# Attention kernel on one core: the value products in two column halves, one ahead of score 1 and one ahead of score 3

## What is computed

```python
q, k, v = jnp.split(qkv, 3, axis=2)
att = jnp.einsum('bhqd,bhkd->bhqk', q, k) / np.sqrt(HEAD_DIM).astype(np.float32)
causal = jnp.tril(jnp.ones((T, T), dtype=bool))
att = jnp.where(causal, att, 0.0)
att = jax.nn.softmax(att, axis=-1)
out = jnp.einsum('bhqk,bhkd->bhqd', att, v)
```

## Time and profile before

| | |
|---|---|
| median of 3 runs | 1096.74 us (1095.18 to 1096.81) |
| the profiled execution's own time | 1100.31 us |
| its span, first to last instruction | 1098.1 us |
| mean granted clock of PE | 0.993 |
| PE busy in the span | 1056.5 us (96%) |
| DVE busy | 843.4 us (77%) |
| ACT busy | 698.0 us (64%) |
| POOL busy | 386.7 us (35%) |

### The profile page before, as it was taken

One profiled execution on the slowest core, in us unless ns is written; L12 is line 12 of the kernel. 1 busy time (PEld: TensorE's weight loads), 2 busy tenths in 40 slices (PEclk: granted clock), 3 DMA queues, 4 the chain that ended last, 5 costly groups with the idle time before them and its releaser, 6 DMA issues.

```text
span 1098.1 us, 21867 instructions
## 1 busy us (share of the span) xinstructions
PE 1056.5 (96%) x8064; PEld 531.2 (48%) x8064; DVE 843.4 (77%) x1185; ACT 698.0 (64%) x1487; POOL 386.7 (35%) x945
## 2 busy tenths in 40 slices
PE   5989999999999999999999999999999999999998
PEld 3655555554544454444444444444454445443445
DVE  5667787679779887988898889879987997798023
ACT  2433333267777777777777777777777777777572
POOL 3211211355414451444253335324531553153301
PEclk9999999999999999999999999999999999999799
DMA  3586664455004600540163036104600460011123
GB/s 126 168 255 184 196 216 151 140 86 95 7 8 64 107 2 14 107 61 7 28 104 44 7 45 108 22 7 60 104 12 8 62 105 7 8 56 37 34 90 120
DMA packets 62030, 84.13 MB, mean 77 GB/s; under 512 B 12260, under 2 KB 42212, under 8 KB 60900
## 3 DMA queue, kind: packets, MB, share of 16 engines
q1 hardware_dynamic: 60772, 78.55, 33.0%
q0 software_dynamic: 1152, 4.19, 1.3%
HBM read 44.30 MB, written 34.08 MB: 71 GB/s over the span
## 4 chain that ended last, share of the span: by engine, by line
PE 76%; DVE 16%; issue 3%; ACT 3%; DMA 1%; POOL 0%; SPq 0%; ACTq 0%; DVEq 0%; POOLq 0%
PE ps_o L1156 21%; PE ps_s L1142 21%; DVE part_max L354 11%; PE ps_m L337 8%; PE ps_vr L736 5%; PE ps_qk L727 4%; PE ps_m L1187 3%; ACT probs L1020 3%; PE ps_o L1167 2%; PE ps_m L344 2%; PE ps_xt L770 2%; PE ps_qk L736 2%; PE ps_s L1131 2%; PE ps_pieces L337 1%; PE ps_s L1132 1%
## 5 line engine op out<-in xcount | busy, mean ns | idle before, releaser
L1020 ACT ACTIVATE probs<-ps_s 128x512 f32<-128x512 f32 (+3 forms) x1280 | 599.4, 538 | 233.4 <-PE ps_s L1142 226.7
L354 DVE TENSOR_REDUCE part_max<-ps_m 128x2 f32<-128x1024 f32 (+2 forms) x594 | 614.4, 1058 | 115.3 <-PE ps_m L337 83.2
L1142 PE MATMUL ps_s<-q_op,k_op 50*128 50x512 f32 (+3 forms) x1280 | 436.2, 424 | 7.1 <-ACT probs L1020 3.0
L337 PE MATMUL ps_m<-k_op,q_op 48*128 48x512 f32 (+3 forms) x1188 | 342.7, 413 | 12.5 <-DVE part_max L354 11.1
L1142 PEld LDWEIGHTS ps_s<-q_op,k_op 50*128 50x128 f32 x1280 | 207.1, 186 | 304.0 <-ACT probs L1020 236.1
L972 POOL TENSOR_SCALAR_AFFINE_SELECT probs<-probs 128x128 f32<-128x128 f32 x512 | 145.8, 294 | 453.5 <-ACT probs L1020 444.9
L1156 PE MATMUL ps_o<-probs,v_sb 128*32 128x512 f32 (+3 forms) x2560 | 302.4, 545 | 0.0
L337 PEld LDWEIGHTS ps_m<-k_op,q_op 48*128 48x128 f32 x1188 | 161.5, 185 | 43.9 <-DVE part_max L354 40.2
L938 POOL TENSOR_TENSOR diag_weight<-ident,masked_weight 128x256 f32<-128x256 f32 x256 | 150.4, 624 | 40.6 <-ACT masked_weight L993 40.6
L344 PE MATMUL ps_m<-mask,pick 64*128 64x64 bf16 (+1 forms) x932 | 91.9, 208 | 0.0
L1156 PEld LDWEIGHTS ps_o<-probs,v_sb 128*32 128x32 f32 x2560 | 50.7, 108 | 72.5 <-issue 31.3
(11 more groups left out here) (76 smaller groups left out, 695.7 us busy)
## 6 DMA issues: line engine op xcount, KB each, us to landing
parts_d<-parts SPq DMA_DIRECT2D x32, 512.0 KB, 4.7
q_op<-parts_d SPq DMA_DIRECT2D x84, 128.0 KB, 7.9
k_op<-parts_d SPq DMA_DIRECT2D x84, 128.0 KB, 8.4
vpad_d<-v_pad SPq DMA_DIRECT2D x32, 256.0 KB, 3.5
v_sb<-vpad_d SPq DMA_DIRECT2D x8, 1024.0 KB, 5.8
x_in<-x SPq DMA_DIRECT2D x8, 512.0 KB, 4.9
ffn_d<-ffn SPq DMA_DIRECT2D x8, 512.0 KB, 3.2
attn_t<-normed SPq DMA_DIRECT2D x128, 32.0 KB, 2.0
```

Of the source, the lines that this page charges most:

```text
L337: last = pe.matmul(ps_m[:, f % ring * 2 + e, 0:width], self.q_op[rows, p, j, q0:q0 + P], self.k_op[rows, p, j, pc * CH:pc * CH + width], s ...
L354: dve.tensor_reduce(both, ps_m[:, bank:bank + 2, 0:width], AX_X, ALU.max).then_inc(self.piece_reduced, 1)
L1020: act.activation(probs[:, slot % PRING, 0:width], ps_s[:, bank_of("scores", slot, i * 2 + p), 0:width], ACT.Exp).then_inc(probs_ready, 1)
L1142: pe.matmul(ps_s[:, bank_of("scores", slot, i * 2 + p), 0:CH - q0], k_op[rows, p, h % 2, kt * P:(kt + 1) * P], q_op[rows, p, h % 2, u * CH ...
```

## The change

A step's order is now written as a string: S a score, M a piece, A and B the two halves of W, X as before. The order before was S M S X S M S W. In the new one A handles the query columns 0 to 255 of the unit and B the columns 256 to 511. A tile is not split when it is the first key tile of its unit or when fewer than 257 of its queries are left; then all of it is done at B and nothing at A. At the first three steps of a unit the weighed tile is one of these.

```diff
+ORDER = "SMASXSMBS"
+
+
+def weighed_columns(u, kt, part):
+
+    q0 = first_query(u, kt)
+    if kt == 0 or q0 >= CH // 2:
+        return (q0, CH) if part == 1 else None
+    return (q0, CH // 2) if part == 0 else (CH // 2, CH)
...
-            def weigh_values(p, u, kt, G):
+            def weigh_values(p, u, kt, G, part):
 
                 n = G * NCH + u
+                if weighed_columns(u, kt, part) is None:
+                    return
...
                 q0 = first_query(u, kt)
+                q1, q2 = weighed_columns(u, kt, part)
                 for at, h in enumerate(HEAD_AT):
-                    last = pe.matmul(ps_o[h * HW:(h + 1) * HW, q0:CH], v_sb[:, p, kt, h * HW:(h + 1) * HW],
-                                     probs[:, ((KT0[u] + kt) * GH + at) % PRING, 0:CH - q0],
+                    last = pe.matmul(ps_o[h * HW:(h + 1) * HW, q1:q2], v_sb[:, p, kt, h * HW:(h + 1) * HW],
+                                     probs[:, ((KT0[u] + kt) * GH + at) % PRING, q1 - q0:q2 - q0],
                                      start=(kt == 0), stop=(kt == key_tiles(u) - 1))
-                last.then_inc(probs_used, 1)
+                if part == 1:
+                    last.then_inc(probs_used, 1)
...
-                        for at in range(GH):
-                            score_tile(u, kt, at, i, p, first, last)
...
+                        at = m = 0
+                        for op in ORDER:
+                            if op == "S":
+                                score_tile(u, kt, at, i, p, first, last)
+                                at += 1
...
+                            if op == "X":
                                 between_scores(i, p, u, kt, first, last)
-                            if at == GH - 1:
-
-
+                            if op in "AB":
+                                part = "AB".index(op)
                                 if kt >= LAG:
-                                    weigh_values(p, u, kt - LAG, G)
+                                    weigh_values(p, u, kt - LAG, G, part)
```

More of the change, by code:

```diff
@@ L1170, in masked_keys, with finish_unit @@
                 last.then_inc(masked_done, 1)
-            def finish_unit(p, u, G, step):
-                weigh_values(p, u, key_tiles(u) - LAG + step, G)
+            def finish_unit(p, u, G, step, part):
+                weigh_values(p, u, key_tiles(u) - LAG + step, G, part)
             def output_tile(k):
@@ new lines, in group @@
+                        for op in ORDER:
+                            if op == "S":
+                                score_tile(u, kt, at, i, p, first, last)
+                                at += 1
+                            if op == "M":
+                                some, ahead = pieces_at(u, kt, m)
+                                m += 1
+                                if not (ahead and last):
+                                    for f in some:
+                                        if ahead and f == 0:
+                                            pe.wait_ge(front_loaded[1 - p], ops.loaded(1 - p, i + 1 + p))
+                                        if ahead and f == PIECE0[NCH // 2]:
+                                            pe.wait_ge(back_loaded[1 - p], ops.loaded(1 - p, i + 1 + p))
+                                        ops.score_piece(pe, ps_m, MRING, f, 1 - p if ahead else p, (G + ahead) * PIECES)
+                            if op == "X":
@@ L1228, in group @@
                                 between_scores(i, p, u, kt, first, last)
-                            if at == GH - 1:
+                            if op in "AB":
+                                part = "AB".index(op)
                                 if kt >= LAG:
-                                    weigh_values(p, u, kt - LAG, G)
+                                    weigh_values(p, u, kt - LAG, G, part)
                                 elif u > 0:
-                                    finish_unit(p, u - 1, G, kt)
+                                    finish_unit(p, u - 1, G, kt, part)
@@ L1236, in group @@
                                 elif not first:
-                                    finish_unit(1 - p, NCH - 1, G - 1, kt)
+                                    finish_unit(1 - p, NCH - 1, G - 1, kt, part)
                 if last:
@@ L1240, in group @@
                     for step in range(LAG):
-                        finish_unit(p, NCH - 1, G, step)
+                        for part in range(2):
+                            finish_unit(p, NCH - 1, G, step, part)
                     for k in range(len(OUT_AT), OUTS):
```

## The result

The changed kernel takes 1089.49 us in the median (1088.02 to 1090.59, 4 runs), the kernel before 1096.78 (1095.18 to 1097.92, 4 runs). The ratio is 0.9934 with a 95% interval of 0.9917 to 0.9951: 7.3 us faster. The forecast was 7.3 us slower, and the time lies 0.5 us under the range's lower end.

The account below looks back on a forecast made before the run. The prediction took a loop of PE and ACT waiting for each other as the bound. Seven groups +3.5, first group's extra +0.6 and last group +3.2 gave +7.3 us: 1096.7 to 1104.0 us, range 1090 to 1113.

Parts of the forecast that it names:

- the blocks: PE's half-row pairs between 128-row operations: one pair alone costs 0.43 us, each further pair 0.24.
- the ring: PE and ACT waiting on each other through 3 score banks: S2 is due 1.24 us after S3, and just fits.
- a plain step: Split step without X: 2.67 us to 2.47 plus masks; thirteen outside steps 6 to 12 give -1.7 a group.
- the 0.14 and 0.18 above: Extra PE time in a plain step: 0.14 us for W's second half, 0.18 for four pairs in two blocks.
- +0.5 us a group: Sum over the 40 steps of a group, between -1.9 and +1.5; +3.5 us for seven groups.
- steps 6 to 12: Stretch of a group set by DVE: PE's new work 17.0 us, DVE's 17.1, taken as 17.5, so -0.6.
- The masks: Mask matmuls of diagonal pieces: nothing extra at 128 columns, 0.05 us more per 128 columns, up to about 0.17.
- They keep a ring wait: Five unsplit steps without X: S2 follows S3 directly and waits until 1.24 us; a full step costs 2.9, together -0.2.
- an argument against a rival: Evenly spaced pieces, 1.24 us apart, set against the rival that DVE is the next bound (1112 us, chance 0.08).
- +7.9 for steps 24 to 39: Last group's steps with an output tile: +7.2 us for steps 27 to 39, +0.24 for each of 24 to 26.
- The -4.9 for the clock: Last group, steps 17 to 23: 24.5 us partly at half clock becomes 19.6 if PE's full clock holds.
- The faster rival: Cheap border between blocks, loads prefetched across it: -1.9 us a group, -10 in all, 1087 to 1092 us; chance 0.21.

Follow-up runs that it names:

- the two kernels with half reductions: The kernel before and the changed kernel, each with VectorE taking the maximum over half of each piece's columns only: 1078.16 and 1083.91 us.
- both pieces together, half reductions: The changed kernel with both pieces behind score 0 (S M M A S X S B S) and VectorE reducing half of each piece's columns: 1096.55 us.

## Why the prediction was wrong, point by point

**The prices of the blocks and the ring: right.** The blocks, the halves and the ring gave a plain step of 2.47 (2.48 measured), a suffix step of about 4.0 (4.07, 3.94, 4.01), steps 17 to 19 of the last group at 2.24 (2.18), steps 17 to 23 at 19.6 (19.4), an output step at 3.49:

```profile
1021.16 0.50 PE L1153 MATMUL ps_s<-q_op,k_op 50*128 50x512 f32 x1
...
1022.77 1.13 PE L1202 MATMUL ps_m<-w_out_sb,attn_t 128*128 128x256 f32 x4
1023.83 0.50 PE L1153 MATMUL ps_s<-q_op,k_op 50*128 50x512 f32 x1
```

(the output tile takes 1023.83 - 1022.77 = 1.06 as before, and the steps 27 to 36 take 3.47 each.) The drain at a change of tiling mode that the Trainium skill states ("TensorEngine Tiling (Array Packing)", Key Properties) agrees with the run of two halves in a row: no change of mode between them, no cost. That page of the Trainium skill gives no size for it; the sizes here are the 0.14 and 0.18 above.

**Where it failed.** The forecast of +0.5 us a group was a difference of larger terms, gains of 2.5 and losses of 3.05; -1.87 came out, 2.4 us lower. Seven groups make 16.6 us of that. By the table above the 2.4 are 1.0 in the five unsplit steps without an X, 0.7 in steps 6 to 12, 0.6 in the plain steps and the small rest in the others.

- *The masks.* "By 0.05 per 128 columns, up to about 0.17" above a block of 0.67. That came from one row, where the masked piece is split over two pairs. In the new order its two halves stand side by side, and a 128-column piece costs 0.07 less than a full one, the widest 0.11 more. For steps 17 and 19 the surcharge was +0.05 and -0.07 was measured, for 18 and 20 +0.28 and +0.14. That is about 0.13 too much for two pieces, some 2 us for the 32 masked pieces of a group, not all of it in steps where PE decides. It is most of the 0.6 in the plain steps, and part of the rest.
- *The first step of a unit.* "They keep a ring wait" is wrong for steps 0, 4, 12 and 24. The S3 in front is on the diagonal with 128 columns; in step 12 its exponential starts at 672.18 and ends at 672.46, 0.64 behind S3's start at 671.82, not 1.2. S2's bank is free early, and the step takes 2.04. The forecast worked out only the full case (2.9, right for step 14 with 2.88) and put the five unsplit steps at -0.2 together; -1.2 was measured, and between the two kernels with half reductions, where DVE hardly counts, still -0.9.
- *DVE as a gain.* In steps 4, 10, 12, 24 and 30 PE of before waits for DVE, 0.15 to 0.6 us each. The forecast saw it in step 30 and in steps 6 to 12, and took the total of DVE's work as the floor of both orders. The even spacing stood in the text only as an argument against a rival. It was worth 2.2 - 0.65 = 1.55 us a group; the classes of the forecast contain some 0.8 of it.
- *The last group.* +7.9 for steps 24 to 39 was 7.1 to 7.6 in the profiles (50.7 + 19.4 against 43.9 + 19.1 with the old order in the last group, and 43.9 + 18.5 in the kernel before). The -4.9 for the clock belonged to one execution: the forecast read a stretch of half clock from one profile, put its end into the difference, and then applied the difference to the median of runs which mostly had none. At an undisturbed clock steps 17 to 23 lose 0.6. Steps 0 to 16 gained 1.6 like the others where +0.2 was forecast.

The errors have opposite signs: seven groups were forecast at +4.1 (with the first group's 0.6) and came to -13.2, the last at +3.2 and came to +6.0. The faster rival had the right sign and size, but for the wrong reason. It wanted a cheap border; the border cost exactly what the rows said.

Of the marks that the forecast named, the plain step, the suffix step and the output step came as forecast. PE's waits for ACT on scores did not fall under 80 us (242.4): that mark was badly chosen, since prefetched loads wait there without any loss.

What stays open: why some executions have a stretch of half clock and most have none. Three of the profiled ones had it in steps 18 and 19 of the last group, one at the start of the first group (the kernel with the old order in the last group) and one in a middle group (both pieces together, half reductions).

## What to carry to other kernels

When an engine and its consumer wait for each other in a ring of buffers, look at when the third party gets its work too: moving a long operation into the middle of a step can gain more by spacing another engine's input than by closing the wait that was aimed at. Count the borders between different tile shapes rather than the instructions, and put operations of the same shape side by side (it is the shape that counts, not only that both use all rows). And where the sum is a small difference of large terms, take the price of each small operation from its neighbourhood in the new order, and no event of a single execution into the difference.

## What the runs showed of the hardware beyond what was expected

- Splitting a product costs nothing that is seen in the step if both parts stand together: 16 matmuls of 256 columns in 1.00 us, as 8 of 512. Apart, each stands between two borders, and a half takes 0.57. A suffix sum beside a half product is a border too (1.07 and 0.56, as beside scores), though both use all 128 rows.
- Two pieces delivered to VectorE 0.24 us apart in place of 1.24, with two buffers, cost 6.6 us in a group against 0.65, at the same 90 us of work, and though it was busy for only 90.15 of 111.57 us.
- The half clock came in some executions of a kernel and not in most, for 10.2 to 20.5 us within the attention stage: in steps 18 and 19 of the last group in three profiled executions, all with the product in one place, in the first group in one, in a middle group in one, and in eight of the thirteen not at all before the closing output tiles.
